# Another order of the statements in the five engines' step loops of an attention and feed-forward kernel

## The chip, the cores and the metric

The kernel runs on one core of a Trainium2 chip. Its time is the device time of one execution in microseconds (us). A kernel is timed in several runs, of which the median is given; one further execution is profiled, and the rows below come from it.

## What is computed

One transformer layer over x of 4 batches, 512 tokens and 256 channels, in float32:

```python
n = layernorm(x)
q = (n @ Wq) in 32 heads of 64;  k, v = (n @ Wk), (n @ Wv) in 8 heads of 64
q, k = rope(q), rope(k)          # rotary positions; each k, v head serves 4 q heads
attn = softmax(causal(q @ k.T / sqrt(64)))
x = x + (attn @ v) @ Wo
q8, in_scale = per_token_int8(layernorm(x))
x = x + float16((q8 @ weight.T) * in_scale * w_scale + bias)
```

## The kernel before

**Tiles and steps.** The 4 batches times 8 key heads make 32 steps (`STEPS`). A step s treats one key head with its 4 query heads over 512 tokens, in 4 query tiles of 128 rows. The program is written out by hand for each of the five engines, as a loop over s: TensorE (PE), ScalarE (ACT), VectorE (DVE), GpSimd (POOL) and SyncE (SP), which issues DMAs. Each engine runs its own statements strictly in the order written; between engines there are semaphores only. So a statement that waits holds up all that stands behind it on its engine.

**One step on PE.** `scores(s, a)` for 11 groups a multiplies queries by keys into one of three score banks: group 0 is query tile 0 (all four heads, 128 keys), groups 1 to 4 are the four heads of the tile with 512 keys, 5 to 8 the tile with 384 keys, 9 and 10 the tile with 256 keys. A group takes the bank of three groups before, and so waits until the exponentials of that group are done. `turn(s, t)` transposes block t of the exponentials (10 blocks), `attend(s, t)` multiplies it by the values, `turn_output(s, v)` transposes the normalised output of query tile v and `out_product(s, v)` multiplies it by Wo. `project(s + 2, j)` computes the two query pairs of the step after next, `project_keys(s + 2)` the keys of two steps at once, in even steps only. In some steps `turn_quant` and `ffn_product` treat a tile of the feed-forward layer.

**One step on ACT and DVE.** `maxima(s, a)` (DVE) finds the row maxima of a score group, `exponentials(s, v, h)` (ACT) exponentiates head h of tile v. `keep_probT` (ACT) and `keep_probT_low` (DVE) copy a turned block from PSUM as a high and a low float16 part. `normalise_output`, `keep_oT` (ACT), `keep_oT_low` (DVE) and `add_product` (DVE) treat the output of a tile.

**The way of a query.** It matters here and goes over four engines. `project(s + 2, j)` on PE; `keep_raw(s + 2, j)` on ACT copies it from PSUM; `swap_halves(s + 2, j)` on SP issues 4 DMAs that swap its halves; `rotate_second`, `rotate_first`, `rotate_sum` on POOL apply the rotary tables; `keep_high` (ACT) and `keep_low` (POOL) split it; `place_queries(s + 2, j)` on SP issues 4 DMAs into the tile qT, two for the high part and two for the low one. The last three stages run in step s + 1. `scores(s + 2, 0)`, which stands in the loop body of step s + 1, waits for all 8 DMAs of both pairs: of the loop body s it is the statement `scores(s + 1, 0)`. Keys go the same way by `keep_raw_keys`, `swap_key_halves`, `rotate_keys_*` and `place_keys`.

In the loop bodies of before, PE runs `scores(s + 1, 0)` behind `project(s + 2, 1)`, near the end of the step; ACT runs the four `exponentials(s + 1, 0, h)` last of all, and `keep_raw(s + 2, 1)` ahead of `keep_oT(s, 2)`:

```python
                keep_high_keys(s + 2)
                keep_raw(s + 2, 1)
                keep_oT(s, 2)
                for h in range(GROUP_HEADS):
                    exponentials(s + 1, 0, h)
```

The wait of `scores` for its queries is this (line numbers of the profile: L767, L768 and L773 are the matmuls of `scores`, L788 of `turn`, L807 of `attend`, L858 of `turn_output`, L644 of every product with split weights, `project` and `out_product` among them; L1022 is `keep_raw`, L1098 `exponentials`, L1110 `keep_probT`, L1123 `keep_oT`, L1453 `keep_probT_low`; L326 the DMAs of `swap_halves`, L359 and L363 of `place_queries`, L307 of `load_wo`; L467 `rotate_second`, L513 `keep_low`):

```python
                if a == 0:
                    pe.wait_ge(keys_placed[s % 2], s // 2 * 64 + 64)
                    for j in range(QUERY_PAIRS):
                        pe.wait_ge(q_placed[j], s * 64 + 64)
```

Of the kernel before, what the change touches and what calls it, by code (L numbers as in the profile page):

```python
# [56 lines left out]
def attention_ffn_kernel(nc: bass.Bass, x: bass.AP, w_group: bass.AP, w_value: bass.AP, w_out: bass.AP,  # L57
# [9 lines left out]
    with ctx:  # L67
# [221 lines left out]
        def _(sp):  # L289
# [25 lines left out]
            def load_ffn_rows():  # L315
                sp.wait_ge(wo_lo, WO_CHUNKS)
                sp.dma_start(fscale, ffn_scale.rearrange("n o -> o n").partition_broadcast(P)).then_inc(rows_loaded, 16)
                sp.dma_start(fbias, ffn_bias.rearrange("(o n) -> o n", o=1).partition_broadcast(P)).then_inc(rows_loaded, 16)
# [65 lines left out]
            swap_halves(1, 1)  # L384
            for s in range(STEPS):
                swap_key_halves(s + 2)
                if s % 2 == 0:
                    load_wo(s + 2)
                    load_wo(s + 3)
                place_queries(s + 1, 0)  # L390
                place_queries(s + 1, 1)
                swap_halves(s + 2, 0)
                swap_halves(s + 2, 1)
                if s == WO_CHUNKS:
                    load_ffn_rows()
                place_keys(s + 2)
                for f in biased_tiles(s - 1):
                    store_tile(f)

            for f in biased_tiles(STEPS - 1):  # L400
                store_tile(f)
# [6 lines left out]
        def _(pool):  # L408
# [185 lines left out]
            for s in range(STEPS):  # L594
                rotate_second(s + 1, 1)
                rotate_first(s + 1, 1)
                rotate_sum(s + 1, 1)
                keep_low(s + 1, 0)
                keep_low(s + 1, 1)
                done_rstd(s)  # L600
                for f in biased_tiles(s):
                    add_bias(f)
                    add_residual(f)
                split_group_weights(s + 3)
                scale_inputs(scaled_tiles(s))
                if s % 2 == 1:
                    keep_wo_low(s + 1)
                    keep_wo_low(s + 2)
                rotate_keys_second(s + 2)
                rotate_keys_first(s + 2)  # L610
                load_group_weights(s + 5)
                rotate_keys_sum(s + 2)
                keep_keys_low(s + 2)
                for f in normalised_tiles(s):
                    normalise_done(f)
                rotate_second(s + 2, 0)
                rotate_first(s + 2, 0)
                rotate_sum(s + 2, 0)
# [8 lines left out]
        def _(pe):  # L627
# [286 lines left out]
            for s in range(STEPS + 1):  # L914
                turn(s, 0)
                scores(s, 4)
                turn_output(s - 1, 3)
                sum_next_weights(s)
                project_keys(s + 2)
                scores(s, 5)  # L920
                scores(s, 6)
                attend(s, 0)
                turn(s, 1)
                turn(s, 2)
                turn_quant(done_tile(s))
                scores(s, 7)
                out_product(s - 1, 3)
                turn_output(s, 0)
                scores(s, 8)
                turn(s, 3)  # L930
                attend(s, 1)
                scores(s, 9)
                ffn_product(done_tile(s))
                turn(s, 4)
                attend(s, 2)
                scores(s, 10)
                project(s + 2, 0)
                turn(s, 5)
                attend(s, 3)
                attend(s, 4)  # L940
                turn(s, 6)
                out_product(s, 0)
                turn_output(s, 1)
                attend(s, 5)
                turn(s, 7)
                attend(s, 6)
                turn(s, 8)
                out_product(s, 1)
                attend(s, 7)
                turn(s, 9)  # L950
                project(s + 2, 1)
                scores(s + 1, 0)
                turn_output(s, 2)
                scores(s + 1, 1)
                attend(s, 8)
                attend(s, 9)
                scores(s + 1, 2)
                out_product(s, 2)
                scores(s + 1, 3)

# [8 lines left out]
        def _(act):  # L969
# [224 lines left out]
            for s in range(STEPS + 1):  # L1194
                exponentials(s, 1, 0)
                exponentials(s, 1, 1)
                keep_probT(s, 0)
                exponentials(s, 1, 2)
                if s % 2 == 1:
                    keep_wo(s + 1)  # L1200
                keep_oT(s - 1, 3)
                exponentials(s, 1, 3)
                keep_raw_keys(s + 2)
                keep_high(s + 1, 0)
                keep_probT(s, 1)
                exponentials(s, 2, 0)
                keep_probT(s, 2)
                exponentials(s, 2, 1)
                keep_oT(s, 0)
                keep_high(s + 1, 1)  # L1210
                exponentials(s, 2, 2)
                keep_probT(s, 3)
                exponentials(s, 2, 3)
                keep_probT(s, 4)
                exponentials(s, 3, 0)
                exponentials(s, 3, 1)
                keep_raw(s + 2, 0)
                keep_probT(s, 5)
                exponentials(s, 3, 2)
                keep_probT(s, 6)  # L1220
                exponentials(s, 3, 3)
                keep_oT(s, 1)
                keep_probT(s, 7)
                if s % 2 == 1:
                    keep_wo(s + 2)
                round_tile(done_tile(s + 1))
                keep_probT(s, 8)
                to_whole(done_tile(s + 1))
                keep_probT(s, 9)
                keep_high_keys(s + 2)  # L1230
                keep_raw(s + 2, 1)
                keep_oT(s, 2)
                if s == STEPS - 1:
                    root(2, slice(LOOP_TILES, LOOP_TILES + 2))
                for h in range(GROUP_HEADS):
                    exponentials(s + 1, 0, h)

            normalise_done(LOOP_TILES + 1)
            root(3, slice(LOOP_TILES + 2, TOK_TILES))
# [10 lines left out]
        def _(dve):  # L1250
# [334 lines left out]
            for s in range(STEPS + 1):  # L1585
                if s < STEPS:
                    normalise_output(s - 1, 3)
                maxima(s, 3)
                maxima(s, 4)
                if s % KV_HEADS == 2:  # L1590
                    for f in maximum_tiles(s):
                        absolute_maximum(f)
                group_scales(s + 2, o_bank, 0)
                keep_probT_low(s, 0)
                keep_oT_low(s - 1, 3)
                maxima(s, 5)
                invert_sums(s, 0)
                maxima(s, 6)
                normalise_output(s, 0)
                keep_quant(done_tile(s))  # L1600
                batch_statistics(s, 0)
                if s == STEPS:
                    finish_root(2, slice(LOOP_TILES, LOOP_TILES + 2))
                    offset_means(2, slice(LOOP_TILES + 1, LOOP_TILES + 2))
                keep_probT_low(s, 1)
                maxima(s, 7)
                keep_probT_low(s, 2)
                add_product(s - 1, 3)
                maxima(s, 8)
                maxima(s, 9)  # L1610
                batch_statistics(s, 1)
                batch_statistics(s, 2)
                scale_product(done_tile(s))
                keep_probT_low(s, 3)
                keep_probT_low(s, 4)
                maxima(s, 10)
                group_maxima(s + 3)
                keep_oT_low(s, 0)
                batch_statistics(s, 3)
                invert_sums(s, 1)  # L1620
                normalise_output(s, 1)
                keep_probT_low(s, 5)
                invert_scales(scaled_tiles(s))
                keep_probT_low(s, 6)
                add_product(s, 0)
                keep_oT_low(s, 1)
                keep_probT_low(s, 7)
                last_statistics(s, 0)
                batch_aggregate(s)
                add_product(s, 1)  # L1630
                invert_sums(s, 2)
                normalise_output(s, 2)
                if s % KV_HEADS == 3:
                    for f in maximum_tiles(s):
                        absolute_maximum(f)
                keep_probT_low(s, 8)
                keep_probT_low(s, 9)
                maxima(s + 1, 0)
                keep_oT_low(s, 2)
                last_statistics(s, 1)  # L1640
                maxima(s + 1, 1)
                invert_sums(s, 3)
                maxima(s + 1, 2)
                if s == STEPS - 1:
                    normalise_output(s, 3)
                    aggregate(LOOP_TILES, LOOP_TILES + 2, TOK_TILES)
# [73 lines left out]
```

## Time and profile before

| | us |
|---|---|
| three timed runs, median (lowest to highest) | 748.58 (748.51 to 749.6) |
| the profiled execution, its own time | 747.3 |
| its span, first to last instruction | 745.1 |
| PE busy in the span | 702.5 |
| DVE busy | 658.8 |
| ACT busy | 634.4 |
| POOL busy | 557.9 |

The span is the time from the first to the last instruction; 2.2 us of the execution lie around it. Matmuls overlap and their ends are modelled, so PE's busy time is no measure of how much room it has; the distance from the start of one matmul to the start of the next is. TensorE's granted clock is at its upper level of 2.4 GHz (0.992 of it in the mean of the span).

### The profile page before, as it was taken

The numbers are of one execution on the slowest core, as the hardware profiler recorded it, in microseconds if no ns is written. First come the engines' busy times: TensorE is split into PE (matmuls) and PEld (weight loads), VectorE is DVE, ScalarE is ACT, GpSimd is POOL, SyncE is SP. The second block draws the span as 40 slices with busy tenths as digits, with TensorE's granted clock in tenths as the row PEclk, the third lists the DMA queues.
The fourth block names the chain that finished last, engine by engine and source line by source line (L and its number), as shares of the span: only waits on it lengthen the run. The fifth ranks groups of instructions, "written<-read, shape, count | busy, mean of one in ns | idle before, by whom it ended". The sixth has DMA issues, their size and how long they took to land.

```text
span 745.1 us, 22980 instructions
## 1 busy us (share of the span) xinstructions
PE 702.5 (94%) x8014; PEld 588.8 (79%) x8014; DVE 658.8 (88%) x1697; ACT 634.4 (85%) x1317; POOL 557.9 (75%) x525
## 2 busy tenths in 40 slices
PE   4889999999999999999999999999999999999993
PEld 3667887878888888888888888888888888888872
DVE  6858999998889989888899898988989988988996
ACT  4778998888889989898889889898898889888883
POOL 4585887787878898787797798778697898777502
PEclk9999999999999999999999999999999999999996
DMA  8233343343334433333333343333433333232300
GB/s 266 57 98 102 73 118 87 83 114 86 87 87 97 85 92 78 87 92 82 86 92 92 94 96 80 87 90 81 96 85 97 87 94 87 67 71 62 86 2 29
DMA packets 56992, 65.80 MB, mean 88 GB/s; under 512 B 12592, under 2 KB 43824, under 8 KB 56880
## 3 DMA queue, kind: packets, MB, share of 16 engines
q1 hardware_dynamic: 53808, 53.85, 30.1%
q0 software_dynamic: 3072, 10.49, 5.1%
q8 instruction: 66, 1.08, 0.7%
q14 instruction: 46, 0.38, 0.2%
HBM read 16.06 MB, written 2.10 MB: 24 GB/s over the span
## 4 chain that ended last, share of the span: by engine, by line
PE 76%; DVE 11%; ACT 8%; issue 3%; DMA 1%; POOL 0%; ACTq 0%; POOLq 0%; DVEq 0%
PE x_bank L644 23%; PE t_bank L788 19%; PE o_bank L807 13%; PE s_bank L767 7%; PE s_bank L768 6%; ACT prob L1098 5%; DVE neg_max L1465 3%; DVE s_bank L1473 2%; PE ot_bank L858 2%; DVE probT L1453 2%; PE s_bank L773 2%; PE t_bank L644 1%; ACT neg_max L1096 1%; DVE value_lo L1323 1%; ACT probT L989 1%
## 5 line engine op out<-in xcount | busy, mean ns | idle before, releaser
L1110 ACT ACTIVATE probT<-t_bank 128x512 f16<-128x512 f32 x320 | 192.1, 600 | 46.3 <-PE t_bank L788 46.3
L1453 DVE SCALAR_TENSOR_TENSOR probT<-t_bank,probT 128x512 f16<-128x512 f32 x320 | 215.2, 686 | 13.5 <-ACT probT L1110 11.4
L788 PE MATMUL t_bank<-ident,prob 128*128 128x128 f32 x1280 | 192.1, 277 | 1.1 <-DVE value_lo L1323 0.7
L1473 DVE CUSTOM_DVE_ANT_0 s_bank<-s_bank,mask_row,score_unit 128x512 f32<-128x512 f32 (+1 forms) x256 | 174.6, 683 | 3.5 <-PE s_bank L768 1.8
L807 PE MATMUL o_bank<-value_hi,probT 128*128 128x65 f16 x2560 | 157.8, 194 | 5.1 <-DVE probT L1453 3.3
L1098 ACT ACTIVATE prob<-s_bank,neg_max 128x512 f32<-128x512 f32 (+1 forms) x256 | 161.2, 645 | 1.2 <-DVE neg_max L1473 1.0
L807 PEld LDWEIGHTS o_bank<-value_hi,probT 128*128 128x128 f16 x2560 | 137.7, 97 | 25.9 <-DVE probT L1453 18.6
L788 PEld LDWEIGHTS t_bank<-ident,prob 128*128 128x128 f32 x1280 | 144.0, 141 | 15.3 <-issue 2.3
L767 PE MATMUL s_bank<-kT,qT 128*128 128x384 f16 (+3 forms) x512 | 140.4, 301 | 11.1 <-ACT prob L1098 7.5
L807 PE MATMUL o_bank<-value_lo,probT 128*128 128x64 f16 x1280 | 141.7, 192 | 0.0
L768 PE MATMUL s_bank<-kT,qT 128*128 128x384 f16 (+3 forms) x512 | 139.3, 299 | 0.0
L644 PE MATMUL x_bank<-xT,wg 128*128 128x512 f32 x468 | 127.5, 407 | 1.0 <-DVE xT L1333 1.0
L644 PE MATMUL x_bank<-wo,oT 128*128 128x256 f32 x768 | 127.3, 301 | 1.1 <-DVE oT L1507 1.1
L807 PEld LDWEIGHTS o_bank<-value_lo,probT 128*128 128x128 f16 x1280 | 117.2, 98 | 5.4
L1098 ACT ACTIVATE prob<-s_bank,neg_max,score_unit 128x128 f32<-128x128 f32 (+1 forms) x256 | 117.0, 510 | 3.2
L467 POOL TENSOR_TENSOR swp<-swp,sin 128x512 f32<-128x512 f32 x64 | 81.8, 1279 | 49.1 <-DMA swp<-raw 48.8
L644 PEld LDWEIGHTS x_bank<-wo,oT 128*128 128x128 f32 x768 | 103.1, 189 | 8.3 <-DVE oT L1507 1.8
L513 POOL TENSOR_TENSOR query_pair<-raw,query_pair 128x512 f16<-128x512 f32 x64 | 74.6, 1165 | 26.7 <-ACT query_pair L1053 26.7
L644 PEld LDWEIGHTS x_bank<-xT,wg 128*128 128x128 f32 x468 | 82.1, 189 | 15.8 <-POOL wg L449 1.4
L475 POOL TENSOR_TENSOR raw<-raw,swp 128x512 f32<-128x512 f32 x64 | 81.8, 1277 | 14.0 <-DVE raw L1349 5.1
L1465 DVE TENSOR_REDUCE neg_max<-s_bank 128x2 f32<-128x512 f32 (+1 forms) x96 | 66.1, 689 | 19.1 <-PE s_bank L773 19.0
L767 PEld LDWEIGHTS s_bank<-kT,qT 128*128 128x128 f16 x512 | 49.0, 97 | 39.4 <-ACT prob L1098 25.1
(146 smaller groups left out, 1151.3 us busy)
## 6 DMA issues: line engine op xcount, KB each, us to landing
swp<-raw SPq DMA_DIRECT2D x320, 64.0 KB, 2.0
qT<-query_pair SPq DMA_DIRECT2D x256, 64.0 KB, 2.1
kT<-key_pair SPq DMA_DIRECT2D x128, 64.0 KB, 2.0
wg_raw<-in_w_group POOLq DMA_DIRECT2D x16, 384.0 KB, 4.0
wg_raw<-in_w_group POOLq DMA_DIRECT2D x16, 256.0 KB, 3.7
resid<-in_x SPq DMA_DIRECT2D x4, 512.0 KB, 8.4
out<-resid SPq DMA_DIRECT2D x16, 128.0 KB, 1.8
wo_stage<-in_w_out SPq DMA_DIRECT2D x4, 256.0 KB, 3.0
```

The source lines that it names most:

```text
L467: nc.gpsimd.tensor_tensor(swp[j][:, :], swp[j][:, :], sin[:, :], ALU.mult).then_inc(rope_second, 1)
L475: nc.gpsimd.tensor_tensor(raw[j][:, :], raw[j][:, :], swp[j][:, :], ALU.add).then_inc(rope_done, 1)
L644: last = nc.tensor.matmul(out_ap, left(a, k), right(b, k), start=(k == 0 and (a, b) == (HI, HI)), stop=(k == n - 1 and (a, b) == (LO, HI)))
L767: nc.tensor.matmul(bank, q, kT[s % 2][:, HI, 0:n], start=(at == 0), stop=False, skip_group_check=True)
L768: last = nc.tensor.matmul(bank, q, kT[s % 2][:, LO, 0:n], start=False, stop=(len(heads) == 1), skip_group_check=True)
L788: last = nc.tensor.transpose(t_bank[B % TURN_BANKS][:, h * P:(h + 1) * P], prob[:, B % PROBS, h, :], ident[:, :])
L807: last = nc.tensor.matmul(o_heads[:, h, 0:columns], probT[B % TURNED][:, a, h, :], part[:, b * Q_TILES + k, g, 0:columns], start=(k == 0 a ...
L1098: nc.scalar.activation(prob[:, slot:slot + blocks, h, :], s_bank[G % SCORE_BANKS][:, at * n:(at + 1) * n].rearrange("p (k n) -> p k n", n= ...
L1110: nc.scalar.activation(turned_half[B % TURNED][HI], t_bank[B % TURN_BANKS][:, :], ACT.Copy, scale=PROB_SCALE).then_inc(probT_hi, 1)
L1453: nc.vector.scalar_tensor_tensor(out=turned_half[B % TURNED][LO], in0=t_bank[B % TURN_BANKS][:, :], scalar=PROB_SCALE, in1=turned_half[B % ...
L1465: nc.vector.tensor_reduce(neg_max[:, s % 2, u:u + len(heads)], s_bank[G % SCORE_BANKS][:, 0:len(heads) * n].rearrange("p (h n) -> p h n", ...
L1473: nc.vector.tensor_tensor_reduce(bank, bank, mask_row[:, SEQ - n:SEQ], score_unit[:, 1, s % KV_HEADS:s % KV_HEADS + 1], UNBOUNDED, ALU.add ...
```

## The change

The loop bodies of the five engines hold the same statements in another order. Nothing else changes: the code ahead of the loops and behind them, each operation, each buffer and each semaphore wait stay. On PE, `scores(s + 1, 0)` goes from behind `project(s + 2, 1)` to behind `turn_output(s, 1)`, ahead of `turn(s, 7)`; `scores(s + 1, 2)` ahead of `attend(s, 8)`; `turn_output(s - 1, 3)` behind `project_keys(s + 2)`. On ACT, the four `exponentials(s + 1, 0, h)` go ahead of `keep_probT(s, 8)`, `keep_oT(s, 2)` ahead of `keep_raw(s + 2, 1)`, and `keep_oT(s - 1, 3)` behind `exponentials(s, 1, 3)`. On DVE, `maxima(s + 1, 0)` goes behind `add_product(s, 0)` and `maxima(s + 1, 2)` ahead of `invert_sums(s, 3)`. On SP, the two `load_wo` go behind `swap_halves(s + 2, 1)`. The core of it:

```diff
 SP
                 swap_key_halves(s + 2)
+                place_queries(s + 1, 0)
+                place_queries(s + 1, 1)
+                swap_halves(s + 2, 0)
...
+                swap_halves(s + 2, 1)
                 if s % 2 == 0:
                     load_wo(s + 2)
                     load_wo(s + 3)
-                place_queries(s + 1, 0)
-                place_queries(s + 1, 1)
-                swap_halves(s + 2, 0)
-                swap_halves(s + 2, 1)
...
 PE
                 scores(s, 4)
-                turn_output(s - 1, 3)
                 sum_next_weights(s)
                 project_keys(s + 2)
+                turn_output(s - 1, 3)
                 scores(s, 5)
...
+                attend(s, 2)
                 turn(s, 4)
-                attend(s, 2)
                 scores(s, 10)
...
                 turn_output(s, 1)
+                scores(s + 1, 0)
+                turn(s, 7)
                 attend(s, 5)
-                turn(s, 7)
                 attend(s, 6)
                 turn(s, 8)
                 out_product(s, 1)
                 attend(s, 7)
                 turn(s, 9)
                 project(s + 2, 1)
-                scores(s + 1, 0)
                 turn_output(s, 2)
                 scores(s + 1, 1)
+                scores(s + 1, 2)
                 attend(s, 8)
                 attend(s, 9)
-                scores(s + 1, 2)
                 out_product(s, 2)
                 scores(s + 1, 3)
...
 ACT
-                keep_oT(s - 1, 3)
                 exponentials(s, 1, 3)
+                keep_oT(s - 1, 3)
                 keep_raw_keys(s + 2)
                 keep_high(s + 1, 0)
...
                 keep_probT(s, 7)
+                for h in range(GROUP_HEADS):
+                    exponentials(s + 1, 0, h)
...
                 keep_probT(s, 8)
                 keep_probT(s, 9)
                 keep_high_keys(s + 2)
+                keep_oT(s, 2)
                 keep_raw(s + 2, 1)
-                keep_oT(s, 2)
...
-                for h in range(GROUP_HEADS):
-                    exponentials(s + 1, 0, h)
...
 DVE
                 add_product(s, 0)
+                maxima(s + 1, 0)
                 keep_oT_low(s, 1)
...
                 keep_probT_low(s, 9)
-                maxima(s + 1, 0)
                 keep_oT_low(s, 2)
+                maxima(s + 1, 1)
+                maxima(s + 1, 2)
                 last_statistics(s, 1)
-                maxima(s + 1, 1)
                 invert_sums(s, 3)
-                maxima(s + 1, 2)
```

The lines left out move work of the feed-forward layer, of the statistics, of Wo's parts and of the keys by a few places within the same loop bodies (on DVE `invert_scales` and `scale_product` ahead of `maxima(s, 9)`, on POOL `scale_inputs` ahead of `keep_low(s + 1, 1)`, on ACT `round_tile` ahead of `keep_raw(s + 2, 0)` and `keep_high(s + 1, 1)` behind `keep_probT(s, 3)`).

## Rows read from the trace of the kernel before

**Rows 1.** The page: busy time of each engine, its share and instructions.

```profile
PE 702.5 (94%) x8014; PEld 588.8 (79%) x8014; DVE 658.8 (88%) x1697; ACT 634.4 (85%) x1317; POOL 557.9 (75%) x525
```

**Rows 2.** PE's timeline at the first `turn` of step 1 and of step 30.

```profile
76.89 0.38 PE L788 MATMUL t_bank<-ident,prob 128*128 128x128 f32 x2
...
691.82 0.38 PE L788 MATMUL t_bank<-ident,prob 128*128 128x128 f32 x2
```

**Rows 3.** PE's timeline around the end of step 14: start, duration, what.

```profile
365.37 0.96 PE L644 MATMUL x_bank<-wo,oT 128*128 128x256 f32 x6
366.17 0.38 PE L858 MATMUL ot_bank<-ident,o_norm 128*128 128x128 f32 x2
366.48 0.20 PE L807 MATMUL o_bank<-value_hi,probT 128*128 128x65 f16 x1
...
371.12 0.23 PE L767 MATMUL s_bank<-kT,qT 128*128 128x128 f16 x1
...
371.80 0.38 PE L858 MATMUL ot_bank<-ident,o_norm 128*128 128x128 f32 x2
372.02 0.38 PE L767 MATMUL s_bank<-kT,qT 128*128 128x512 f16 x1
...
373.41 1.06 PE L644 MATMUL x_bank<-wo,oT 128*128 128x256 f32 x6
374.62 0.39 PE L767 MATMUL s_bank<-kT,qT 128*128 128x512 f16 x1
...
376.14 0.33 PE L767 MATMUL s_bank<-kT,qT 128*128 128x384 f16 x1
...
376.93 0.34 PE L767 MATMUL s_bank<-kT,qT 128*128 128x384 f16 x1 [0.29 <-ACT prob L1098]
...
377.55 0.20 PE L807 MATMUL o_bank<-value_hi,probT 128*128 128x65 f16 x1
```

**Rows 4.** ACT's timeline around the end of step 14.

```profile
371.32 0.69 ACT L1022 ACTIVATE raw<-x_bank,proj_scale 128x512 f32<-128x512 f32 x1 [0.28 <-PE x_bank L644]
372.22 0.47 ACT L1123 ACTIVATE oT<-ot_bank,pow_rows 128x256 fp32r<-128x256 f32 x1 [0.21 <-PE ot_bank L858]
...
376.76 0.48 ACT L1123 ACTIVATE oT<-ot_bank,pow_rows 128x256 fp32r<-128x256 f32 x1
377.11 0.70 ACT L1098 ACTIVATE prob<-s_bank,neg_max 128x512 f32<-128x512 f32 x1
```

**Rows 5.** SP's timeline of the DMA issues for step 16's queries.

```profile
372.04 2.41 SPq L326 DMA_DIRECT2D swp<-raw  x4
...
381.19 1.10 SPq L363 DMA_DIRECT2D qT<-query_pair  x2
...
383.62 1.23 SPq L363 DMA_DIRECT2D qT<-query_pair  x2
```

**Rows 6.** POOL's timeline of step 16's queries.

```profile
376.13 1.26 POOL L467 TENSOR_TENSOR swp<-swp,sin 128x512 f32<-128x512 f32 x1
...
380.01 1.16 POOL L513 TENSOR_TENSOR query_pair<-raw,query_pair 128x512 f16<-128x512 f32 x1
```

**Rows 7.** DMA issues of the page: count, KB, median us to landing.

```profile
swp<-raw SPq DMA_DIRECT2D x320, 64.0 KB, 2.0
qT<-query_pair SPq DMA_DIRECT2D x256, 64.0 KB, 2.1
```

**Rows 8.** DMA from 384.5 to 386.5 us: queue (packets, MB, share), issues as above.

```profile
q8 instruction: 1, 0.02, 3.4%
...
qT<-query_pair SPq DMA_DIRECT2D x1, 64.0 KB, 2.7
```

**Rows 9.** SP's timeline in step 0.

```profile
62.30 0.58 SPq L307 DMA_DIRECT2D wo_stage<-in_w_out  x1
...
68.39 1.23 SPq L363 DMA_DIRECT2D qT<-query_pair  x2
```

**Rows 10.** PE's timeline: the first matmul of `turn_output(0, 1)`.

```profile
67.91 0.27 PE L858 MATMUL ot_bank<-ident,o_norm 128*128 128x128 f32 x1
```

## What the change should do to the time

> **What bounds the kernel now.** I read the page first. PE is busy for 94% of the span [rows 1], but its busy time is modelled, so I went on to PE's timeline and took the distance from one start to the next. There PE is seen to stream with hardly a gap: from 366.48 to 371.80, for instance, nine statements follow each other without a wait [rows 3]. The steps 1 to 29 take 691.82 - 76.89 = 614.93 us, or 21.20 us each [rows 2]. So PE sets the pace, and the change, which adds and removes no operation, can only touch the few places in a step where PE stands still. There are four, and all show around the end of step 14 [rows 3]:
>
> - between `out_product(s, 2)` and `scores(s + 1, 3)`: 373.41 to 374.62 is 1.21 us. The same product with nothing holding up its follower takes 365.37 to 366.17, 0.80. So 0.41 us are a wait for the exponentials of group 0, whose bank group 3 takes;
> - between `scores` 5 and 6: 376.14 to 376.93 is 0.79 us, of which two matmuls of 384 columns fill 0.33: 0.46 us;
> - between `scores` 6 and `attend` 0: 376.93 to 377.55 is 0.62, less 0.33: 0.29 us;
> - between `turn_output(s, 1)` and `attend` 5: 366.17 to 366.48 is 0.31, less 0.22 (the `turn_output` at 371.80 is followed after 0.22): 0.09 us.
>
> The waits on the exponentials are the largest item of PE in the waits view [rows 2]. The second and the third place stand still in odd steps only: in even steps `project_keys` lies ahead of them and hides them. So an even step loses 0.50 us, an odd one 1.25.
>
> **What the change takes away.** With `scores(s + 1, 0)`, its maxima and its exponentials moved up by some 5 us, group 3 finds its bank free: 0.41 us gone in every step. `attend` 5 comes behind two more statements: 0.09 gone. The stalls of odd steps mostly stay. They hang on a chain that starts at the end of `turn_output(s, 2)` and runs `keep_oT`, `keep_oT_low`, `maxima` 1 and 2, `add_product`, `normalise_output`, `maxima` 3, `exponentials(1, 2)`; it takes 4.91 us now (372.02 to 376.93 [rows 3]), and its members are the same after. What PE itself does in that stretch is 4.91 - 0.41 - 0.46 = 4.04. I leave 0.76 of the 0.87 standing, and half of the 0.29: an odd step gains 0.09 + 0.11 + 0.15 = 0.35, an even one 0.50, the mean is 0.42. If nothing new came in, 29 steps would give 12.2 us.
>
> **What it adds: a wait for the queries.** `scores(s + 1, 0)` needs the eight DMAs of `place_queries(s + 1)`. In before it stands behind `project(s + 2, 1)`, at 371.12, and never waits for them. After, it stands at the end of `turn_output(s, 1)`, in step 14 at 366.17 + 0.22 = 366.39, 4.73 us earlier [rows 3]. When do the queries land? In the step after this one, for step 16, the last of the DMAs starts its issue at 383.62 + 0.62 = 384.24 [rows 5] and lands 2.7 us later [rows 8], at 386.94. The new place of `scores` in that step is one step, 21.20 us in the mean, behind 366.39, at 387.59, so with the old chain it would just do. But the chain itself moves. `scores` now stands ahead of `project(s + 2, 1)`, so a wait of `scores` delays the next step's queries, and it closes a loop: from `scores(s + 1, 0)` over the second query pair back to `scores(s + 2, 0)`, one step later. Its links, each from a row:
>
> - PE, from `scores(s + 1, 0)` to the end of `turn_output(s, 2)`: all the statements between 366.48 and 371.80, 5.32 us (they are the same, `scores` now first), and 0.22: 5.54 [rows 3].
> - ACT: 0.20 until `keep_oT(s, 2)` starts (372.02 to 372.22), 0.35 until the next can (376.76 to 377.11), 0.69 for `keep_raw(s + 2, 1)`, which stands behind it in the new order: 1.24 [rows 3, 4].
> - SP: the four issues of `swap_halves`, 2.41 us for four, so the last begins after 1.81 [rows 5], 0.03 after the ACT instruction's end (372.01 to 372.04 [rows 4, 5]), and 2.0 to landing [rows 7]: 3.84.
> - POOL, from `rotate_second` at 376.13 to the end of `keep_low(16, 0)` at 381.17: 5.04 [rows 6].
> - SP: from there to the last of the six issues that are left, at 384.24: 3.07 [rows 5, 6].
> - Landing: between 2.1, the median [rows 7], and 2.7, the case in which a packet of code is fetched at the same time [rows 8].
> - Hand-overs between engines that the links leave out (DMA to POOL, DMA to PE): 0.10, as three of the 0.03 above.
>
> Without the landing this is 5.54 + 1.24 + 3.84 + 5.04 + 3.07 + 0.10 = 18.83. With 2.1 it is 20.93 us a step, a little under the 21.20 of now; with 2.7, 21.53. The code packet holds one DMA engine for 3.4% of 16 engines times 2 us, 1.09 us [rows 8], so the top end is 2.1 + 1.09: 22.0. PE's own work without this wait is 21.20 - 0.42 = 20.78, so at every one of these values the loop, not PE, would set the step. I take 2.6 for the landing, close to the row with the packet, since that packet follows PE's place in the program and the queries' DMAs lie in the same part of the step as now; a little less than 2.7, as the issues of odd steps move against it. That gives 21.43 us a step, 0.23 more than now: 29 x 0.23 = 6.7 us.
>
> The Trainium skill, page "DMA: Bandwidth & Descriptors", section "Queues, rings and completion order", says that a DMA engine serves its queues in turn and changes only between packets, and its section on why a DMA counts 16 says that only the full count means landed; by that a DMA would be as late as the one engine that is busy with code, in every step, which is the 22.0. The landing of 2.7 [rows 8] agrees in kind, though not with the whole packet.
>
> In even steps SP has four more DMAs ahead of these (`swap_key_halves`, 2.4 us by the same rows), while POOL is still in its 5.04; I put them at nothing, and at 0.4 a step in even steps where they aren't covered, 6 us, which is inside the range.
>
> **Step 0.** The last query DMA begins at 68.39 + 0.62 = 69.01 [rows 9]; the two `load_wo`, 0.58 each, now go behind it, so 67.85, and it lands 2.1 to 2.7 later, at 70.0 to 70.6. `scores(1, 0)` would stand at 67.91 + 0.22 = 68.13 [rows 10]: a wait of 1.8 to 2.4, less the 0.50 saved. I take +1.6.
>
> **The rest, at nothing.** `turn_output(s - 1, 3)` behind `project_keys`: its output is needed by `out_product(s - 1, 3)`, covered by `attend` 0 and two `turn`. `scale_product` and `invert_scales` ahead of `maxima(s, 9)` can make DVE wait for `ffn_product` or for POOL in a few steps; what waits behind is `exponentials(s, 3, 0)`, for which ACT is not yet free. The four exponentials ahead of `keep_probT(s, 8)` take slots in which ACT waits for PE. The attends and turns that swap places use other banks' data of long before. Without their cover each would cost some tenths in a quarter of the steps, 2 or 3 us in all.
>
> **Sum.** Against the profiled execution of 747.3: + 6.7 + 1.6 = 755.6. The median of the runs is 748.58, 1.28 above, so 756.9; I write 757.
>
> **The rivals.**
>
> - *The queries are in time.* If a link is shorter than I read it (POOL's start is hidden, SP's issues run faster), or the DMAs land by `turn_output`'s end, only the gains stay: 748.58 - 12.2 = 736.4. For it: the landing in before, at 386.94, is ahead of the new place at 387.59. Against it: the new order of `keep_oT` and `keep_raw` adds 0.57 to the loop (0.22 for `turn_output`, 0.35 for `keep_oT`), and the sum has to fall by 0.65 us to 20.78. This is the case of the other side; it decides from a loop under 21.15 on. Chance 0.20.
> - *The loop binds, but at its floor*, each landing at 2.1 as the median has it: 29 x (20.93 - 21.20) + 1.6 = -6.2, so 742. Against it: the queries' last DMAs meet a code packet in the row that I have. Chance 0.12.
> - *Each landing is late by the whole packet*: 29 x (22.02 - 21.20) + 2 = +25.8, so 774. For it the code packet's length, against it the 2.7 measured. Chance 0.18.
> - My forecast, landings between 2.4 and 2.9, 748 to 766: chance 0.50.
>
> **Range and chances.** The range from 738 to 773 leaves out most of the first rival and the upper half of the third. A measurement of this kernel tells about 0.2%, 1.5 us, from no change. Faster: the first two rivals, 0.32, of which I give 0.02 to no change; same: this and the lowest end of the forecast, 0.07; slower: 0.63. The range of the likeliest case alone is 748 to 766.
>
> **What the profile after would show.** Right: in the waits, PE or PEld of `scores` (L767) waiting for DMA qT<-query_pair in nearly every step, some 0.5 to 1 us each; even and odd steps of about the same length, 21.4; no wait of `scores` 3 on ACT; ACT without its idle time ahead of `keep_probT(s, 8)`. Wrong: no wait for qT at all, and steps of 20.8 us in the mean; then the loop has been read too long. Also wrong: a new wait at `attend` or `turn` on DVE in every step, which would mean that DVE's order, not the queries, sets the step.

## The result and the profile after

The new order is slower. Its median is 771.47 us (769.4 to 775.79, 4 runs) against 748.55 (747.64 to 749.6) for the order before, a ratio of 1.0313 [1.0264, 1.0363]: 22.9 us more, where 8.4 were forecast. The profiled execution took 769.4 us, its span is 767.3. Runs more than 1.5% above the fastest of their kernel are left out of the medians and ratios of this document: one of run 5 (806.78 us), one of run 11 (2791.57) and one of the order before beside run 5 (885.4).

I read the same views as before. The page's busy row, against [rows 1]: every engine does the same work, in a longer span.

```profile
PE 701.5 (91%) x8014; PEld 595.0 (78%) x8014; DVE 650.4 (85%) x1697; ACT 642.0 (84%) x1317; POOL 557.7 (73%) x525
```

PE's timeline at the first `turn` of step 1 and of step 30, against [rows 2]: 712.88 - 78.47 = 634.41 us for 29 steps, 21.88 each instead of 21.20. That is 634.41 - 614.93 = 19.5 of the time lost, 0.67 a step.

```profile
78.47 0.60 PE L788 MATMUL t_bank<-ident,prob 128*128 128x128 f32 x4
...
712.88 0.49 PE L788 MATMUL t_bank<-ident,prob 128*128 128x128 f32 x3
```

PE's waits from 200 to 700 us (what waited, for what, us in all, times, longest): queries, which PE of before is not seen to wait for in this view. Its largest item there is the last line.

```profile
PE s_bank L767 <- DMA qT<-query_pair: 14.0, 15, 1.6
PE s_bank L767 <- ACT prob L1098: 11.5, 19, 1.4
...
PE s_bank L767 <- ACT prob L1098: 4.4, 17, 0.3
```

The view puts a wait for several semaphores down to one of them and so names the queries only 15 times. By the records of the DMAs, `scores(s + 1, 0)` starts 0.14 us behind the last landing of its queries in every one of the steps 1 to 28; in before it is 3.3 to 5.2 us. I also took the distance from start to start, statement by statement over all steps, and subtracted that of before. The loop took 21.2 us more from its first to its last PE statement. From `turn_output(s, 1)` to what follows it, now `scores(s + 1, 0)`, it is 30.0 us more; from `out_product(s, 2)` to `scores(s + 1, 3)` 12.8 less; from `scores(s + 1, 2)` to what follows it 5.4 more; everything else together is 1.4 less. One such place, on PE's timeline: `turn_output(14, 1)` takes 0.22, and `scores(15, 0)` starts 1.50 behind its start.

```profile
378.68 0.38 PE L858 MATMUL ot_bank<-ident,o_norm 128*128 128x128 f32 x2
380.18 0.22 PE L767 MATMUL s_bank<-kT,qT 128*128 128x128 f16 x1 [1.12 <-DMA qT<-query_pair]
```

The chain that ended last, by engine, says the same: SP, DMA and POOL hold a third of it, where in the same view of before (second line) PE alone has 76%.

```profile
PE 47%; SPq 13%; DMA 10%; POOL 9%; ACT 7%; DVE 7%; issue 6%; ACTq 0%; POOLq 0%; DVEq 0%
...
PE 76%; DVE 11%; ACT 8%; issue 3%; DMA 1%; POOL 0%; ACTq 0%; POOLq 0%; DVEq 0%
```

**The loop, link by link.** These are the links of the forecast, each as the mean of 28 steps (1 to 28), from the records of the instructions and of the DMAs. A step s of the loop runs here from `scores(s + 1, 0)` to `scores(s + 2, 0)`, over the queries of step s + 2:

| link | forecast | measured |
|---|---|---|
| PE, `scores(s+1,0)` to the end of `turn_output(s,2)` | 5.54 | 5.45 |
| ACT, to the end of `keep_raw(s+2,1)` | 1.24 | 1.25 |
| SP, to the start of the last `swap_halves` | 1.84 | 1.87 |
| its landing | 2.0 | 2.12 |
| POOL, to the end of `keep_low(s+2,0)` | 5.04 | 5.05 |
| SP, to the start of the last `place_queries` | 3.07 | 3.68 |
| its landing | 2.6 | 2.24 |
| hand-overs, DMA to POOL and DMA to PE | 0.10 | 0.07 + 0.14 |
| sum | 21.43 | 21.85 |

(The rounded links add up to 21.87.) PE stood still for the queries 33.0 us in 31 steps, 1.06 a step, where the forecast has 21.43 - 20.78 = 0.65.

**Where the excess lies.** The links run from event to event, so they add up to a step by their definition. That the loop holds no slack shows in their spread: in all 28 steps PE's link is 5.43 to 5.46, ACT's 1.25, POOL's 5.04 to 5.07, and both hand-overs stay the same. With the shortest values of the other four, 1.84, 2.03, 3.09 and 2.03, the loop would take 20.95, and steps 22 and 24 do take 20.97 and 20.98. The mean lies 0.90 above this floor: 0.59 in the link to the last issue, 0.20 in its landing, 0.09 in the landing of `swap_halves` and 0.02 in the link ahead of that. The link to the last issue runs from 3.09 to 4.62 in steps 8 to 28, and the landing behind it from 2.03 to 3.22. SP's timeline shows what happens. Ahead of the wait above, in step 13, from `keep_low(15, 0)` on, two issues that take 1.23 elsewhere took 2.59:

```profile
373.46 2.59 SPq L363 DMA_DIRECT2D qT<-query_pair  x2
376.16 1.18 SPq L359 DMA_DIRECT2D qT<-query_pair  x2
377.38 1.23 SPq L363 DMA_DIRECT2D qT<-query_pair  x2
```

The DMA view of 373.4 to 376.2 (queue, packets, MB, share of 16 engines) has one code packet in it: 3.3% of 16 times 2.8 us, 1.48 us on one engine.

```profile
q1 hardware_dynamic: 236, 0.19, 31.8%
q8 instruction: 1, 0.02, 3.3%
```

Nine steps later the packet is over by then, and all issues are even:

```profile
570.47 1.10 SPq L363 DMA_DIRECT2D qT<-query_pair  x2
571.67 1.18 SPq L359 DMA_DIRECT2D qT<-query_pair  x2
572.89 1.24 SPq L363 DMA_DIRECT2D qT<-query_pair  x2
```

In steps 8 to 28, from the end of `keep_low` to the last landing it is 5.12 or 5.13 us in three steps (22, 24, 28), whose packet began 0.4 to 0.9 us ahead of that end and held up no issue, and 5.36 to 6.65 in the 18 others. In each of the 18 one issue is stretched, to between 0.72 and 1.96, where 0.60 is usual; in step 23, whose packet began 0.4 us ahead too, it is an issue just ahead of that end, of 1.74 us. In three of the 18 (steps 10, 11, 17) it is the last one, and then the time appears in the landing, which is counted from its start. The packets are 16 KB and take 0.9 to 1.5 us. All of SP's issues for queries and keys from 200 to 700 us say the same: of those during which a packet was under way 20 of 48 took over 0.68 us, of the others 1 of 456. In before it is 25 of 71 and 0 of 447. That the packet is the cause is read from this coincidence; no run moved the packets alone.

### The profile page after: what moved, and what is told of

Read it like the earlier page. It is cut to its first block, busy times and chain, and to the rows that moved or that the text cites. A ratio compares the mean times of both kernels' runs of the same rounds, so it can differ in the third digit from the quotient of the medians.

```text
span 767.3 us, 22980 instructions
## 1 busy us (share of the span) xinstructions
PE 701.5 (91%) x8014; PEld 595.0 (78%) x8014; DVE 650.4 (85%) x1697; ACT 642.0 (84%) x1317; POOL 557.7 (73%) x525
## 4 chain that ended last, share of the span: by engine, by line
PE 47%; SPq 13%; DMA 10%; POOL 9%; ACT 7%; DVE 7%; issue 6%; ACTq 0%; POOLq 0%; DVEq 0%
PE x_bank L644 15%; PE t_bank L788 10%; PE o_bank L807 8%; DMA qT<-query_pair 6%; SPq L363 5%; PE s_bank L767 5%; DMA swp<-raw 4%; SPq L359 4%; PE s_bank L768 4%; SPq L326 3%; POOL swp L467 2%; POOL raw L461 2%; POOL query_pair L513 2%; POOL raw L475 2%; DVE s_bank L1473 2%
## 5 line engine op out<-in xcount | busy, mean ns | idle before, releaser
L1110 ACT ACTIVATE probT<-t_bank 128x512 f16<-128x512 f32 x320 | 189.2, 598 | 35.6 <-PE t_bank L788 32.9
L1453 DVE SCALAR_TENSOR_TENSOR probT<-t_bank,probT 128x512 f16<-128x512 f32 x320 | 211.9, 684 | 5.0 <-ACT probT L1110 4.8
L1098 ACT ACTIVATE prob<-s_bank,neg_max 128x512 f32<-128x512 f32 (+1 forms) x256 | 158.2, 635 | 24.3 <-DVE neg_max L1473 22.6
L1473 DVE CUSTOM_DVE_ANT_0 s_bank<-s_bank,mask_row,score_unit 128x512 f32<-128x512 f32 (+1 forms) x256 | 169.4, 682 | 3.3 <-PE s_bank L768 3.3
L807 PE MATMUL o_bank<-value_hi,probT 128*128 128x65 f16 x2560 | 152.3, 194 | 2.8 <-DVE probT L1453 2.8
L807 PE MATMUL o_bank<-value_lo,probT 128*128 128x64 f16 x1280 | 138.4, 192 | 0.0
L644 PE MATMUL x_bank<-xT,wg 128*128 128x512 f32 x468 | 129.7, 413 | 1.0 <-DVE xT L1333 1.0
L644 PE MATMUL x_bank<-wo,oT 128*128 128x256 f32 x768 | 124.1, 297 | 1.1 <-DVE oT L1507 1.1
L1098 ACT ACTIVATE prob<-s_bank,neg_max,score_unit 128x128 f32<-128x128 f32 (+1 forms) x256 | 120.4, 511 | 3.2
L644 PEld LDWEIGHTS x_bank<-wo,oT 128*128 128x128 f32 x768 | 100.7, 189 | 3.3 <-DVE oT L1507 1.3
```

Source lines behind the costliest of these rows:

```text
L644: last = nc.tensor.matmul(out_ap, left(a, k), right(b, k), start=(k == 0 and (a, b) == (HI, HI)), stop=(k == n - 1 and (a, b) == (LO, HI)))
L807: last = nc.tensor.matmul(o_heads[:, h, 0:columns], probT[B % TURNED][:, a, h, :], part[:, b * Q_TILES + k, g, 0:columns], start=(k == 0 a ...
L1098: nc.scalar.activation(prob[:, slot:slot + blocks, h, :], s_bank[G % SCORE_BANKS][:, at * n:(at + 1) * n].rearrange("p (k n) -> p k n", n= ...
L1110: nc.scalar.activation(turned_half[B % TURNED][HI], t_bank[B % TURN_BANKS][:, :], ACT.Copy, scale=PROB_SCALE).then_inc(probT_hi, 1)
L1453: nc.vector.scalar_tensor_tensor(out=turned_half[B % TURNED][LO], in0=t_bank[B % TURN_BANKS][:, :], scalar=PROB_SCALE, in1=turned_half[B % ...
L1473: nc.vector.tensor_tensor_reduce(bank, bank, mask_row[:, SEQ - n:SEQ], score_unit[:, 1, s % KV_HEADS:s % KV_HEADS + 1], UNBOUNDED, ALU.add ...
```

## The experiments

Each kernel was timed beside the order before on the same chip. The ratios are to that order; the differences in us are between medians. The order after was timed once; the median of before lay between 747.64 and 748.55 each time.

**1 and 2: the move of group 0 and the rest, each alone.** Run e1 is the order after with `scores(s + 1, 0)`, its maxima and its exponentials in their old places, e2 the order before with these three moved:

```diff
 e1, from after (e2 does the reverse, from before)
 PE    turn_output(s, 1)
-      scores(s + 1, 0)
       ...
       project(s + 2, 1)
+      scores(s + 1, 0)
 ACT  -exponentials(s + 1, 0, h)    # ahead of keep_probT(s, 8)
      +exponentials(s + 1, 0, h)    # last of the loop body
 DVE  -maxima(s + 1, 0)             # behind add_product(s, 0)
      +maxima(s + 1, 0)             # behind keep_probT_low(s, 9)
```

> The changed order, but scores(s + 1, 0), maxima(s + 1, 0) and the four exponentials(s + 1, 0, h) stand where they stood before the change; all other moves stay. Theory of the query loop (scores ahead of project waits for the queries' DMAs and passes its wait on to the next step's queries): the wait of scores on DMA qT is gone, steps of about 21.2 us again, 745 to 752 us. Rival (the other moves cost: keep_oT ahead of keep_raw, turn_output behind project_keys, DVE's and SP's new orders): the time stays above 762 us.

> The kernel before, with scores(s + 1, 0), maxima(s + 1, 0) and the four exponentials(s + 1, 0, h) alone moved to where the change puts them. Query loop: the same wait on DMA qT appears, but keep_raw still stands ahead of keep_oT, so the loop is 0.57 us shorter than after the change: 21.3 us a step, 752 to 758 us. Rival (the other moves cost): no slower than before, 736 to 748 us.

Measured: e1 773.8 us, ratio 1.0349 [1.0333, 1.0364]; e2 783.57, 1.0494 [1.0451, 1.0537]. Both expectations fell; for e1 the rival held, that the other moves cost, for e2 neither. With neither part it is 748.5 us, with the rest alone 773.8, with group 0 alone 783.6, with both 771.5: the parts do not add up.

In e1 there is no wait for queries, as the loop has it, but the stall ahead of `scores` 3 is 12.2 us longer than before; the 5.4 us behind `scores` 2 show here too. ACT's timeline of e1 shows why. In before `keep_raw` runs while PE is still at `scores(s + 1, 0)` [rows 4]. Here ACT is idle for 1.18 us ahead of `keep_oT`, which waits for `turn_output(s, 2)`, and runs `keep_raw` only after it; the exponentials of group 0 stand behind both.

```profile
383.41 0.47 ACT L1123 ACTIVATE oT<-ot_bank,pow_rows 128x256 fp32r<-128x256 f32 x1 [1.18 <-PE ot_bank L858]
383.78 0.68 ACT L1022 ACTIVATE raw<-x_bank,proj_scale 128x512 f32<-128x512 f32 x1
```

So `keep_oT` ahead of `keep_raw`, to which I gave a price only in the loop, also holds up these exponentials where they do not go ahead too. Of the 26.1 us that the loop of e1 takes more, 4.6 lie between `attend` 6 and `turn` 8, as in run 4 (5.2); the waits view names no engine there, and the cause stays open. The rest that run 1 keeps has more in it than the list of the change says: on ACT the exponentials of tiles 2 and 3 change places with copies of turned blocks, on DVE `maxima(s, 10)`, `keep_oT_low` and `add_product` move.

In e2 the queries' wait is there (25.5 us more behind `turn_output(s, 1)`), with a loop of 22.2 us. Its ACT link is the short one of 0.67 in 17 of 28 steps only (0.93 to 1.46 in the others), POOL starts 0.5 to 0.6 late in every second step from step 4 on, and the link to the last issue is 3.98; what lengthens them was not tested. To that, 6.4 us come ahead of `scores` 6 and 4.7 ahead of `attend` 9.

**3: `keep_raw` first.** After, with one pair of lines swapped back:

```diff
-                keep_oT(s, 2)
                 keep_raw(s + 2, 1)
+                keep_oT(s, 2)
```

> The changed order with keep_raw(s + 2, 1) ahead of keep_oT(s, 2) again. Query loop: it loses turn_output's 0.22 and keep_oT's 0.35 us, 0.57 us a step or 16 us: 753 to 759 us, even though keep_oT, and with it oT and the output product, come 0.6 us later. Rival (the queries are late for another reason, by landings alone): within 4 us of 771.5.

Measured: 768.71, ratio 1.0279 [1.0264, 1.0295]. The raw link fell from 1.25 to 0.67, as expected, and the wait for queries by 7.4 us; but `scores` 6 starts 3.9 us later in all, since `keep_oT` heads the chain to it. The loop is as long as after, 21.85 in the mean of steps 1 to 28: the issue link (3.85 against 3.68), the last landing (2.48 against 2.24) and smaller waits took back what the raw link gave. The loops of the two profiled executions differ by 0.2 us, so the 2.8 between the medians are not clear of noise. The expectation missed; the time is where the rival had it, though the raw link did what I said.

**4: a later place for group 0.** After, with the three statements further back, so that the queries have time:

```diff
 PE    turn_output(s, 1)
-      scores(s + 1, 0)
       turn(s, 7)
       ...
       turn(s, 8)
+      scores(s + 1, 0)
 ACT   exponentials(s + 1, 0, h): from ahead of to behind keep_probT(s, 8)
 DVE   maxima(s + 1, 0): to behind keep_probT_low(s, 7)
```

> The changed order with scores(s + 1, 0) behind turn(s, 8) instead of behind turn_output(s, 1), maxima(s + 1, 0) behind keep_probT_low(s, 7), and the four exponentials behind keep_probT(s, 8). Query loop: turn 7, attend 5, attend 6 and turn 8 (1.6 us) leave the loop, 21.9 - 1.6 = 20.3 us, which is less than PE's own 20.8, so the wait on DMA qT nearly goes and the gain of the early exponentials stays: 736 to 744 us. Rival (early group 0 costs by crowding ACT and DVE): no faster than 755 us.

Measured: 755.86, ratio 1.012 [1.01, 1.014], 15.6 us less than after. `scores` now starts 0.14 to 1.64 us behind the landing of its queries, 0.94 in the mean, and PE's waits from 200 to 700 no longer have them:

```profile
PE s_bank L767 <- ACT prob L1098: 6.4, 12, 0.6
PE x_bank L644 <- DVE resid L1517: 0.6, 3, 0.2
```

So the wait for queries is what makes after slow. That the order then ends 8 us above before, not below it, is what the expectation missed, and where the rival had it: of 27.1 us that go behind `turn_output(s, 1)`, 13.4 come back in other places, the most of it (5.2) between `attend` 6 and `turn` 8.

**5 and 6: one DMA more.** One SP DMA of 64 KB, from `q_hi` into a tile that nothing reads, is added to each `place_queries(s + 1, 1)`; it comes on top of the computation. Run e5 adds it to after, e6 to before:

```diff
+                if j == 1:
+                    if s:
+                        sp.wait_ge(spare_done, 16 * s)
+                    sp.dma_start(spare[:, :], q_hi[0:64, :]).then_inc(spare_done, 16)
```

> The changed order with one DMA more a step on SP: place_queries(s, 1) copies 64 rows of the query pair's high part into a spare tile between its high and its low DMAs; nothing reads the spare tile. Query loop: one more issue of 0.63 us lies in the loop, so each step is 0.6 us longer, 29 steps 18 us: 786 to 793 us. Rival (the wait is a matter of landings, which the issue overlaps): within 5 us of 771.5.

> The kernel before with the same one DMA more a step. Query loop: before the change the queries land some 4 us ahead of scores, so it costs nothing: 746 to 750 us. Rival (SP or the DMA engines are near a limit in both kernels): slower by 5 us or more.

Measured: e5 796.89 (792.3 to 800.33), ratio 1.0644 [1.0569, 1.0719], slower than expected; e6 747.99, 1.0002 [0.999, 1.0014], as expected. The same DMA costs nothing before and 25.4 us after: SP's issues are on the loop of after and not on that of before. The price is above the 0.6 a step of an issue that I expected. The link to the last issue grew by 0.91, from 3.68 to 4.59, and the landing behind it fell by 0.15. Of the 26.9 us that the loop of the profiled execution takes more than after, 22.3 show behind `turn_output(s, 1)` and 4.7 in the five statements that follow. TensorE's granted clock, at its upper level all through the loop of after, falls to 1.2 GHz three times there, for 3.4 us each, right behind waits for the queries of 2.15 to 2.29 us; behind a wait of 2.40 it did not. So a part of the price, up to those 4.7 us, is the clock and not SP.

**7 and 8: the later place, built on before.** Run e7 moves group 0 behind `turn(s, 8)` in before, as in run 4, with `keep_oT` ahead of `keep_raw`; e8 also moves three statements ahead of `scores` 6:

```diff
 e8, from e7
 PE   -turn_output(s - 1, 3)      # behind scores(s, 4)
      +turn_output(s - 1, 3)      # behind scores(s, 5)
 DVE  -normalise_output(s - 1, 3) # ahead of maxima(s, 3)
      +normalise_output(s - 1, 3) # behind maxima(s, 3)
      -maxima(s, 4)               # ahead of keep_probT_low(s, 0)
      +maxima(s, 4)               # behind it
```

> The kernel before with scores(s + 1, 0) behind turn(s, 8), maxima(s + 1, 0) behind keep_probT_low(s, 7), the four exponentials behind keep_probT(s, 8), and keep_oT(s, 2) ahead of keep_raw(s + 2, 1). Query loop: here the queries land about 1 us ahead of scores, as in the run of the changed order with the same place, so no wait on DMA qT; the 0.41 us ahead of scores 3 goes in each step, and turn 7 and attend 5 stand as before: 738 to 745 us. Rival (early exponentials crowd ACT and give the gain back): 747 us or more.

> As the kernel with group 0 behind turn 8 in the old order, and besides the chain from turn_output(s, 2) to attend 0 is cut: on DVE maxima 3 stands ahead of normalise_output(s - 1, 3), and keep_probT_low(s, 0) ahead of maxima 4; on PE turn_output(s - 1, 3) stands behind scores 5. If that chain of DVE and ACT sets the rest of the odd steps' stalls, another 0.3 us in each odd step go, 4 us below that kernel. Rival (it does not matter, or what is put back is late next): the same as that kernel, or slower.

Measured: e7 757.11, ratio 1.0123 [1.0102, 1.0144]; e8 773.51, 1.0351 [1.0333, 1.0368]. Both miss, on the side of their rivals. In e7 there is no wait for queries, and the loop still takes 11.4 us more than before; the stall ahead of `scores` 3 is 11.0 shorter, but `attend` 8 to 9 is 7.5 longer and `scores` 5 to 6 4.1. The view of PE's waits names DVE for the first, the low parts that now stand behind the maxima:

```profile
PE o_bank L807 <- DVE probT L1453: 3.6, 13, 0.3
```

In e8 the stalls ahead of `scores` 6 and `attend` 0 are gone (5.1 and 5.4 us less than before), but from `attend` 0 to `turn` 1 it is 25.2 us more: the stall went one place on.

**9: one link on POOL.** After, with `keep_low` of pair 0 between the two rotations of pair 1, so that SP gets the first low part earlier:

```diff
                 rotate_second(s + 1, 1)
+                keep_low(s + 1, 0)
                 rotate_first(s + 1, 1)
                 rotate_sum(s + 1, 1)
-                keep_low(s + 1, 0)
```

> The changed order, with keep_low(s + 1, 0) on POOL between rotate_second(s + 1, 1) and rotate_first(s + 1, 1). POOL's work in the query loop stays 5.05 us, but the last keep_low then has only two DMA issues behind it instead of six: the link of 3.7 us from keep_low to the last issue and the waits in it shrink by about 0.4 us a step. Query loop: 12 us faster, 756 to 763 us. Rival (not POOL and SP but the landings set the wait): within 4 us of 771.5.

Measured: 760.31, ratio 1.017 [1.0153, 1.0187], as expected. One statement of an engine that idles for a quarter of the span takes 11.2 us off the kernel; 13.1 us of PE's standing still behind `turn_output(s, 1)` go, and no other place changes by more than 1.4. PE's wait for queries from 200 to 700, 14.0 us in after, is here:

```profile
PE s_bank L767 <- DMA qT<-query_pair: 8.3, 15, 1.2
```

**10: e1 with the exponentials first.** ACT's four exponentials of group 0 go ahead of `keep_raw`, directly behind `keep_oT(s, 2)`:

```diff
                 keep_oT(s, 2)
+                for h in range(GROUP_HEADS):
+                    exponentials(s + 1, 0, h)
                 keep_raw(s + 2, 1)
```

> As e1_group0_back (773.8 us), with the four exponentials(s + 1, 0, h) directly behind keep_oT(s, 2), ahead of keep_raw(s + 2, 1) and to_whole. If e1 is slow because these two stand ahead of the exponentials that scores 3 waits for, the 0.66 to 1.06 us ahead of scores 3 shrink by 0.6 us and more a step: 752 to 758 us. Rival (e1 is slow by the other moves, at turn 7 and turn 8 or at scores 6): 768 us or more.

Measured: 800.92, ratio 1.0719 [1.0696, 1.0741], a clear miss. The stall ahead of `scores` 3 went (24.8 us less than in e1), so `keep_raw` and `to_whole`, ahead of the exponentials, did hold it up. But `out_product(s, 2)` now waits for the bank that `keep_raw` has still to empty, 1.69 us in steps 0 to 29:

```profile
PE x_bank L644 <- ACT raw L1022: 33.5, 22, 1.5
```

**11 and 12: two further cuts on top of 9.** Run e11 is e9 with `keep_raw` ahead of `keep_oT` (the edit of run 3); e12 is e9 with `scores(s + 1, 0)` one statement later, behind `turn(s, 7)`.

> The order after, with POOL's keep_low of pair 0 between the two rotations of pair 1 (which gave 760.3) and ACT's keep_raw ahead of keep_oT (which alone gave 2.8 us). Loop theory: PE still waits 0.46 us a step for the queries (0.24 in even steps, 0.70 in odd ones); the raw link falls by 0.57, so even steps wait no more and odd ones 0.15 to 0.3, some 9 us less; against that stand the 4 us that keep_raw first adds ahead of scores 6. 753 to 757. Rival (the wait is no longer what sets the end, PE's own stalls are): 758 to 762.

> The order after, with keep_low moved as before and PE's scores(s+1,0) one statement later, behind turn 7. Loop theory: the place comes 0.44 us later, so that nearly all the wait in even steps and some 0.4 of it in odd ones is filled with turn 7; 10 us less than 760.3: 748 to 753. Rival (maxima and exponentials of group 0, whose places stay, now come late and hold up the probT copies behind them, as they did with scores behind turn 8): 755 to 761.

Measured: e11 765.07, ratio 1.023 [1.0209, 1.0252]; e12 759.15, 1.0145 [1.013, 1.0161]. e11 misses both theories. Its raw link fell by 0.58, but for the queries of even steps POOL then waits for ACT's `keep_high`, and the wait for queries stays at 0.48 a step (steps 9 to 29; 0.46 in e9); the 4.0 us ahead of `scores` 6 come on top. POOL's waits from 200 to 700, 20.6 us in e9, are in e11:

```profile
POOL query_pair L513 <- ACT query_pair L1053: 34.2, 44, 1.7
```

e12 went as the rival says: 12.8 us less behind `turn_output(s, 1)`, 7.2 more behind `turn` 8 and 5.7 more behind `turn` 7, where `scores(s + 1, 0)` now stands. No other order that I ran beats the order before; the nearest is run 4, 755.86.

## Why the prediction was right and wrong

**Right: what sets the step.** The wait for `qT`, nearly every step, in the place named, and a loop that closes over the second query pair. Run 4 takes the wait away and gives back 15.6 us, run 9 shortens one link and gives 11.2, run 5 lengthens one and costs 25, while the same DMA costs nothing in before.

**Wrong: the size, by the terms of SP and the DMAs.** Where no packet of code is in the way, the loop is as forecast: 20.95 us against 20.93 with the landing at 2.1. The step that failed is what the packet adds. I put 0.5 a step, as a landing of 2.6, "since that packet follows PE's place in the program and the queries' DMAs lie in the same part of the step as now", and nothing on SP's issues: "to the last of the six issues that are left, at 384.24: 3.07" comes from one step in which nothing held SP up [rows 5, 6]. Measured are 0.90 a step, 0.59 of it in that link. The DMAs did not stay in their part of the step: in steps 8 to 28 the packet begins 3.3 us behind the end of `keep_low` in before, in the median, and 0.4 in after. So it meets the issues, and stretches one of them, where in step 14 of before it met the landing [rows 8].

In the terms of the sum: 3.68 + 2.24 = 5.92 against my 5.67, and 1.87 + 2.12 = 3.99 against 3.84 for the swap; with the hand-overs, 0.21 against 0.10, that is 0.25 + 0.15 + 0.11 = 0.51 more, and PE's link gives 0.09 back. 0.42 of a step, the difference of the sums. The period rose by 0.67 a step where I had 0.23: 29 x 0.44 = 12.8 of the 14.5 us that I missed. The rest: 0.8 in step 30 and 0.3 in step 31, which I did not count, and 0.8 because after's profiled execution lies 2.1 under its median, before's 1.3. Step 0 rose by 0.6 instead of 1.6, and the loop began 0.96 later, for which I have no cause.

That the result still lies inside 738 to 773 is owed to the third rival, which adds the whole packet, 1.09, to each landing and ends at 774. Its size is nearer to the 0.90 than my 0.5 was, but not its mechanism: the landings took 2.24 in the mean, not 3.19.

The Trainium skill, page "DMA: Bandwidth & Descriptors", section "Queues, rings and completion order", has a DMA engine change queues only between packets; by that I let the packet delay a landing. The traces agree in part. In steps 8 to 28 of before, 8 of the 21 last landings take 2.68 to 3.39 though their issue takes 0.60, with a packet that begins 0.4 to 1.1 us after the issue did. In after the last landing takes 2.03 to 2.05 in 18 steps, and longer (2.84 to 3.22) in the three whose last issue is stretched too. There the delay is seen at the issue, and the rule alone does not give that.

**Wrong without effect: the gain at `scores` 3.** I read 1.21 - 0.80 = 0.41 us as a wait [rows 3]. PE's timeline of before, just ahead of it:

```profile
373.17 0.38 PE L767 MATMUL s_bank<-kT,qT 128*128 128x512 f16 x1
373.38 0.38 PE L768 MATMUL s_bank<-kT,qT 128*128 128x512 f16 x1
373.41 0.47 PE L644 MATMUL x_bank<-wo,oT 128*128 128x256 f32 x1
```

The first matmul of `out_product` is recorded 0.03 behind the second of `scores`, whose distance to a follower is 0.21 or 0.22 at the other `scores` of 512 columns in before. So 0.18 of the 0.41 were work of `scores` 2. After, with `attend` in between, it shows there: the 5.4 us more behind `scores` 2. By this the true gain of this place is 12.8 - 5.4 = 7.4 us, and all gains together 30.0 - 21.2 = 8.8 instead of 12.2. While the loop sets the step, they do not count; the rival in which the queries are in time would have ended at some 740, not 736.4.

**The rest, at nothing.** In after, it holds: no place but those named changes by more than 2.3 us over the loop. As a statement about the parts, it fails: run 1 has the rest alone at 26 us, most of it because ACT's new order holds up the exponentials of group 0. The edits lean on each other.

**Smaller points.** Even and odd steps were to be alike at 21.4; they are 22.00 and 21.47 (steps 8 to 29). `scores` 3 no longer waits for ACT, as said. The view of waits that the prediction names with [rows 2] is not in those rows; its line of before stands in the section on the result. Settled by the runs are the wait and the loop; open are the packets as the only cause of the longer links, and the reason why a later place for group 0 costs 8 to 9 us in other stalls (runs 4 and 7), which I read from the traces but did not test.

## What to carry to other kernels

When a statement moves ahead of the producer of its own next input, look for the loop that this closes over the engines, add up its links, and take each from many steps: the mean of SP's link was 0.6 above the one step that I read. A stall is measured from start to start over both statements around it, since a matmul may be recorded as started while the one ahead still streams. And an engine that idles for a quarter of the span can carry the link that sets the step: moving one POOL statement was worth 11 us.

## What was not expected of the hardware

A fetch of code, a single packet of 16 KB that takes 0.9 to 1.5 us on one DMA engine, coincides with a stretched DMA issue on SP, 0.72 to 1.96 instead of 0.60, in 18 of 21 steps of after; I had expected late landings, which before shows where the packet begins behind the issue. One more SP DMA of 64 KB, whose issue takes 0.6, lengthened SP's link of the loop by 0.91. And behind three waits of PE of 2.15 to 2.29 us TensorE's granted clock fell to 1.2 GHz for 3.4 us.
